# Sums of squares of two weight halves on ScalarE instead of Gram products on TensorE, in an adaptive-norm mixture-of-experts kernel

## The reference, cut to what matters

```python
out = einsum('bsi,io->bso', Efou * ys[:, None, :], weight) * d[:, None, :]
router_logits = y @ router_w.T + router_b + 0.1 * expert_weights
top_p, top_i = top_k(softmax(router_logits), 2)
top_p = top_p / top_p.sum(axis=-1, keepdims=True)
h = gelu(einsum('bsd,edh->bseh', y, w1) + b1, approximate=False)
expert_out = einsum('bseh,ehd->bsed', h, w2) + b2
x = x + (top_p[..., None] * take(expert_out, top_i)).sum(axis=2)
```

## Time and profile before

| what | value |
|---|---|
| median of 3 runs | 298.06 us (297.62 to 298.10) |
| the profiled execution | 296.99 us |
| its span | 295.2 us |
| its mean granted clock of TensorE | 0.965 of full |
| busy: PE / DVE / ACT / POOL | 269.6 / 191.9 / 195.2 / 175.4 us |
| read / written in HBM | 27.61 / 9.64 MB |

### The profile page before, as it was taken

The page is one execution under the profiler, slowest core; times in us unless marked ns, Lnnn a source line. Parts: engine busy times, 40 slices in busy tenths (PEclk is TensorE's granted clock), DMA queues, the critical chain, the costliest instruction groups (busy, mean ns, idle before and its releaser), DMA issues.

```text
span 295.2 us, 8972 instructions
## 1 busy us (share of the span) xinstructions
PE 269.6 (91%) x3065; PEld 221.2 (75%) x3065; DVE 191.9 (65%) x430; ACT 195.2 (66%) x425; POOL 175.4 (59%) x160
## 2 busy tenths in 40 slices
PE   7899967899999999999999999999999989999800
PEld 5778957788799998877778777777777767877500
DVE  2957787799999897656655655555656555556510
ACT  3355469499897997677667676766776756776500
POOL 8200026833366989887777877767787657464340
PEclk9799996999999999999999999999999999999985
DMA  6799995499862234645535555534535434332220
GB/s 160 290 400 388 368 323 155 129 404 450 294 191 41 38 59 69 95 76 88 93 56 91 75 93 73 79 68 76 90 59 80 88 56 74 53 39 25 32 35 1
DMA packets 39881, 39.53 MB, mean 134 GB/s; under 512 B 19920, under 2 KB 35744, under 8 KB 39680
## 3 DMA queue, kind: packets, MB, share of 16 engines
q1 hardware_dynamic: 32320, 28.56, 31.7%
q0 software_dynamic: 7488, 10.39, 21.9%
q10 hardware_dynamic: 32, 0.01, 0.0%
HBM read 27.61 MB, written 9.64 MB: 126 GB/s over the span
## 4 chain that ended last, share of the span: by engine, by line
PE 73%; DVE 9%; issue 6%; DMA 5%; POOL 4%; ACT 0%; DVEq 0%; POOLq 0%
PE ps L639 30%; PE ps L656 28%; DVE wsp L940 5%; PE ps L537 5%; DMA out<-onehot,idx 4%; PE ps L555 3%; POOL out L468 2%; PE ps L648 1%; POOL onehot L459 1%; PE ps L479 1%; PE ps L615 1%; DMA rows<-y_rows,idx 1%; PE ps L510 1%; PE ps L519 1%; DVE dv L871 1%
## 5 line engine op out<-in xcount | busy, mean ns | idle before, releaser
L639 PEld LDWEIGHTS ps<-onehot,wsp 128*128 (+1 forms) x1872 | 130.0, 98 | 37.4 <-issue 2.9
L639 PE MATMUL ps<-onehot,wsp 128*128 128x128 f16 x1872 | 154.4, 219 | 1.8 <-issue 1.5
L818 ACT ACTIVATE pay<-ps,cur 128x128 f32<-128x128 f32 x312 | 117.5, 463 | 54.9 <-issue 39.9
L656 PE MATMUL ps<-wsp,pay 128*128 (+1 forms) x616 | 139.4, 316 | 1.2 <-DVE pay L1102 1.2
L468 POOL DMA_INDIRECT out<-onehot,idx x39 | 68.7, 1762 | 28.9 <-POOL onehot L459 12.1
L1102 DVE SCALAR_TENSOR_TENSOR pay<-pay,cur 128x512 f16<-128x512 f32 x72 | 54.9, 762 | 28.8 <-ACT pay L806 26.6
L437 POOL DMA_INDIRECT rows<-y_rows,idx x39 | 49.4, 1266 | 22.4 <-issue 11.0
L459 POOL TENSOR_SCALAR onehot<-onehot,cur 128x256 f32<-128x256 f32 x37 | 43.0, 1161 | 25.6 <-DVE onehot L1120 21.6
L656 PEld LDWEIGHTS ps<-wsp,pay 128*128 128x128 f16 x616 | 45.3, 97 | 5.0 <-issue 1.6
L1096 DVE TENSOR_SCALAR pay<-pay,cur 128x512 f16<-128x512 f32 x36 | 19.4, 538 | 26.4 <-ACT pay L818 24.1
L806 ACT ACTIVATE pay<-pay,cur 128x512 f16<-128x512 f32 x36 | 26.0, 722 | 1.2
(11 more groups left out here) (177 smaller groups left out, 193.0 us busy)
## 6 DMA issues: line engine op xcount, KB each, us to landing
stage<-in_L_ffn_w SPq DMA_DIRECT2D x9, 1024.0 KB, 9.9
wsp<-in_L_ffn_w SPq DMA_DIRECT2D x7, 1024.0 KB, 11.8
y_rows<-pay SPq DMA_DIRECT2D x4, 512.0 KB, 9.4
wsp<-in_x SPq DMA_DIRECT2D x3, 512.0 KB, 8.1
b2bc<-in_L_ffn_b SPq DMA_DIRECT2D x1, 1024.0 KB, 9.4
rows<-y_rows,idx POOLq DMA_INDIRECT x39
out<-onehot,idx POOLq DMA_INDIRECT x39
wsp<-in_x SPq DMA_DIRECT2D x2, 256.0 KB, 5.8
```

The costliest lines, as they stand in the source:

```text
L639: last = mm(ps[:, HB + (2 * j + g) % RING, c * P:(c + 1) * P], wsp[:, bass.ds(e, 1), o:o + P].rearrange("p a f -> p (a f)"), xsp[:, j % RI ...
L656: last = mm(ps[:, OB + j % 2, 0:width], hsp[:, (2 * j + g) % NH, part, c, :], wsp[:, bass.ds(e, 1), o + w:o + w + width].rearrange("p a f ...
L818: last = a.activation(to, ps[:, HB + (2 * j + g) % RING, c * P:(c + 1) * P], ACT.Gelu, bias=cur[:, j % CURS, cc:cc + 1], scale=cur[:, j % ...
```

## The change

Group 6 (halves 14 and 15) has no Gram product any more. ACT squares each half as it lies in its place, 2048 float32 in a partition, with a running sum into its column of wsum: half 14 in turn 3, half 15 in turn 4, each in ACT's program ahead of that turn's split_high. PE drops gram(6) and DVE drops gram_max(6). At the end of turn 4 PE waits for both squares (and for the earlier users of the bank), then does sum_squares(6), and DVE does scale_weights(6) behind rows_out and low_h of turn 4, the place in its program where it was before. The sum is now the whole sum of squares of a half, where it was a sum of row maxima of the Gram product.

```diff
-GRAMS = {4: 4, 7: 5, 9: 6}
+GRAMS = {4: 4, 7: 5}
+SQUARED, SQUARES, SCALES = 6, {7: (14,), 9: (15,)}, 10
...
+        sqjunk = sb("sqjunk", [P, HALF], F8)
...
             def sum_squares(g):
-                if g < EARLY_GROUPS:
+                if g == SQUARED:
+                    pe.wait_ge(w_squared, len(GROUPS[g]))
+                elif g < EARLY_GROUPS:
...
                 if 2 * j + 2 in GRAMS:
                     gram(GRAMS[2 * j + 2])
+                if 2 * j + 2 == SCALES:
+                    for h in range(SQUARED):
+                        if GRAM_BANKS[h] == GRAM_BANKS[SQUARED]:
+                            pe.wait_ge(w_raw if h < EARLY_GROUPS else w_scaled[h], h + 1 if h < EARLY_GROUPS else 1)
+                    sum_squares(SQUARED)
...
+            def squares(n):
+                act.wait_ge(w_in[PLACE[n]], 16 * (len(earlier(n)) + 1))
+                k = column(n)
+                a.activation(sqjunk[:, :], staged_flat(n), ACT.Square, accum_out=wsum[:, k:k + 1],
+                             saturate=False).then_inc(w_squared, 1)
...
                 if j + 2 < XACT:
                     copy_x(j + 2)
+                for n in SQUARES.get(2 * j + 1, ()):
+                    squares(n)
                 for n in HIGHS.get(2 * j + 1, ()):
                     split_high(n)
...
                 if 2 * j + 2 in GRAMS:
                     gram_max(GRAMS[2 * j + 2])
+                if 2 * j + 2 == SCALES:
+                    scale_weights(SQUARED)
```

More of the change, by code:

```diff
@@ L239, in adaln_moe @@
         te_ready = sem("te_ready")
-        w_sq = sem("w_sq"); w_max = sem("w_max"); w_raw = sem("w_raw"); w_rounded = sem("w_rounded")
+        w_sq = sem("w_sq"); w_squared = sem("w_squared"); w_max = sem("w_max"); w_raw = sem("w_raw"); w_rounded = sem("w_rounded")
         gram_done, w_psum, w_scaled, w_t = (
```

## The result

| | before | changed |
|---|---|---|
| median, first measurement | 297.84 us (4 executions, 297.35 to 298.10) | 302.42 us (4, 301.06 to 304.52) |
| median, the run after_again below | 298.39 us (35, 296.21 to 301.23) | 303.06 us (12, 299.42 to 305.10) |
| the profiled execution | 296.99 us, span 295.2 | 301.06 us, span 299.3 |

The change makes the kernel slower: ratio 1.0162, 95% interval 1.0091 to 1.0232, in the first measurement, and 1.0112, 1.0070 to 1.0154, in the second. The direction was forecast, the size was not: 300.2 us was predicted and 302.0 was the upper end.

What follows compares the result with a forecast made beforehand. PE was taken to bound the kernel, with ACT's nearly solid program leaving no slack at two PE waits. The median 298.06 plus PE's shift of 2.1 us, which includes 1.0 from turn 3, gave 300.2 us; range 299.0 to 302.0.

Steps and rivals of the forecast that it cites:

- What bounds the kernel: PE's chain, with two waits without slack: gram_max(5) before sum_squares(5), 0.05 us; split_low(14) before tile 7's up matmuls, none.
- The price of a square: ACT, turns 3 and 4: each square with its accumulator read takes 2.0 us start to start, ends 1.9 and 2.2.
- The wait for half 14: ACT, turn 3: the square of half 14 waits 0.9 us for its load, ends 0 and 1.5.
- Step 1: Turn 3: split_high(12) moves by 2.9 us, PE waits 2.85 at sum_squares(5) and is 1.0 late after turn 4.
- Step 2: Turns 4 to 6: PE waits another 1.0 us for a late split_low(14); its shift becomes 2.1 us.
- What follows turn 6: After tile 7's first up matmuls: split_low(15) has 2 us to spare, so nothing is added.
- After 112 us: PE is busy 142.41 of 144 us at full clock, so its turn 6 shift is the end's shift.
- The clock: Turn 3: PE's 2.85 us idle may bring 6.8 us of half clock, costing 0.7 or 2.4 more; chance 0.25.
- The range: Whole kernel: 299.0 us with no load wait and cheap squares, to 302.0 with long ones and 0.5 for the clock.
- W: ACT's wait in turn 3 for half 14's load, ahead of its square: 0.9 us, ends 0 and 1.5.
- rival on the clock: Slower still, by half clock after PE's idle time in turn 3: 300.9 us, up to 302.6; chance 0.25.
- The base: Whole kernel before the change: median 298.06 us, 1.07 above the profiled execution, to which the shift was added.

Runs made afterwards that it cites:

- after_again: The changed kernel unedited, measured once more for its scatter; median 303.06 us over 12, ratio to before 1.0112.
- no_squares: The changed kernel without its two squares, sum_squares(6) adding group 5's columns instead; median 297.88 us, ratio to before 0.9970.
- filled: The changed kernel with eleven dummy matmuls in PE's program just ahead of sum_squares(5); median 300.91 us, ratio to before 1.0079.
- first_square_behind: Against the changed kernel: only half 14 squared, behind split_high(12) in turn 3, half 15 keeping its Gram product; median 299.48 us, ratio 1.0044.
- after_third: The changed kernel unedited, run for a further profile; 215.67 us from gram(5) to the end.
- layout_only: The kernel before with the added tensor and semaphore declared but never used; median 298.51 us, ratio to before 0.9998.
- squares_behind: The changed kernel with each square behind that turn's split_high instead of ahead; median 299.16 us, ratio 1.0018.
- squares_added: The kernel before, gram(6) and gram_max(6) kept, with the two squares added at the change's places, results unread; median 305.02 us, ratio 1.0228.
- first_square_only: Against the changed kernel: only half 14 squared, ahead of split_high(12), half 15 keeping its Gram product; median 304.93 us, ratio 1.0220.
- squares_twice: The kernel filled, here with 20 dummy matmuls, with each square done twice; four times from 302.08 to 308.30 us, ratio to before 1.0195.

## Why the prediction was wrong in size

- **What bounds the kernel: right.** Both points without slack were the ones named, and a third was missed (below). no_squares shows the second from the other side: PE's saving alone runs into split_low(14).
- **The price of a square: right.** 1.91 us from start to start against 2.0.
- **The wait for half 14: right in the first profile, wrong as a range.** 0.88 against 0.9. But over the profiles with the square ahead of the split, ACT's idle before it was 0.57 to 2.5 us, and I had 0 to 1.5, from two loads of one execution. Most of it goes to PE through gram_max(5), but not all: with 0.95 us more in after_again sum_squares(5) came 0.52 us later than in the first profile, with 1.33 more in filled 0.91, since ACT had come to the square earlier against gram(5) there.
- **Step 1: right.** split_high(12) moved by 2.90 us against gram(5) (82.55 - 82.84 = -0.29 before, 86.81 - 84.20 = 2.61 after), 2.9 forecast. PE was 13.14 - 12.09 = 1.05 us late after turn 4, 1.0 forecast.
- **Step 2: right in its result, partly by luck.** The second wait was 1.12 us long, 1.0 forecast; PE's shift at tile 7's up product is 20.31 - 18.14 = 2.17 us, 2.1 forecast. Inside it two misses cancel: split_low(14) started 2.51 us late against gram(5) (98.23 - 82.84 = 15.39 before, 102.10 - 84.20 = 17.90 after), 2.3 forecast, and it took 2.35 us where I had something between that and 2.69.
- **What follows turn 6: the step of the sum that failed, +0.5.** "I add nothing for it" looked at split_low(15) alone, and "nothing behind takes a delay in" was taken to cover the rest. At tile 8's up product the shift is 2.73 us, with PE idle for 0.40 us on issue. PE's register load for tile 8's expert (line L297 before, L299 after) starts at 105.5 us before and at 109.7 after, each time about 0.5 us behind the end of DVE's copy_x(8) (105.1 and 109.2). PE's transposes of tile 9 wait for that copy, and the load stands behind them, so a late copy leaves no time to do it under the matmuls. That is read from two timelines; filled has 0.21 us of the same idle time, and no run took the load away.
- **After 112 us: right for the changed kernel.** 2.73 us at tile 8 are 2.66 at the end. It is not exact in general: no_squares lost 0.4 and first_square_behind 0.5 us between tile 8 and the end.
- **The clock: the chance was wrong, the mechanism right, the price too high.** The prediction gave the fall 0.25; two of the three profiles of the changed kernel have it. It also said that the wait in turn 6 hides most of what the fall costs, and that is so: turn 4 took 2.67 us longer in after_again and the end was an estimated 1.1 us later for the fall of 6.8 us, where 2.4 was forecast, and 0.1 later for the fall of 3.4 in after_third, where 0.7 was forecast.
- **The range: the other step that failed.** Its upper end of 302.0 had W up to 1.5 (measured up to 2.5) and 0.5 for the clock, although the prediction's own rival on the clock went to 302.6, so the range did not hold what the text held possible. And it had no term at all for what happens ahead of gram(5), where the three profiles of the changed kernel lie 1.36, 3.00 and 3.85 us behind the one profile that served as base. Of the 1.96 us by which the profiled execution missed its forecast (301.06 against 299.1), 1.36 lie there and 0.56 behind gram(5).
- **The base.** 298.06 was the median of three; that of 35 is 298.39. That is 0.3 of the miss.

An estimate for the medians, from the table: 298.4 + 3.3 (from gram(5) on, the middle one of the three profiles: 2.7 as in the first, 0.6 more for a later half 14 and a short fall) = 301.7 us, against 303.06 measured (302.42 in the first four executions). The 1.4 us left lie ahead of gram(5). Whether the change has a hand in them is open. layout_only says that the layout has none. The same sum for squares_behind and filled, whose programs are the same as the changed kernel's up to turn 3, leaves -0.5 and -0.7 us, which speaks for chance; no run took the scatter of the start away.

## What to carry to other kernels

A share of busy time says nothing about whether an engine can take more work: look at what stands behind the place of the new instruction in the same queue, and how long before its reader each of those ends. ACT, at 66% and off the chain, had 0.05 us to give ahead of split_high(12) in turn 3, and behind it the square cost PE no wait there. When a forecast contains an idle stretch of PE of several microseconds, take the half clock after it as likely and not as a tail, look for later waits that hide its cost, and take the scatter of the base from dozens of executions before giving a range of one per cent.

## What the runs showed of the hardware that I had not expected

- In five profiles PE waited long at sum_squares(5) with nothing to do. A wait of 2.73 us (the first profile of the changed kernel) left the clock at 2.4 GHz. With waits of 2.41 us (squares_added), 3.24 (after_again), 3.28 (after_third) and 3.93 (first_square_only) it fell to 1.2 GHz, for 6.8, 6.8, 3.4 and 3.4 us, so the length of the wait decides neither whether it falls nor for how long. In first_square_only it fell only at 92.4 us, 1.3 us after the wait had ended. In the six profiles without a wait of over 0.9 us in turns 3 and 4 it did not fall there. The Trainium skill, page "TensorE: Matmul & The Clock Gate", section "HAM oscillation — how this bites in real kernels", warns of idle gaps of PE from which it returns cold. The traces agree in four of the five. In the profiles of filled and squares_twice, with dummy matmuls in the wait, it did not fall.
- The start varies by itself: in the profiles of all versions gram(5) starts anywhere from 82.56 to 87.24 us, 4.7 us apart, which is more than the change costs from gram(5) on in any of its three. The time at half clock before it goes from 3.4 us (filled) to 20.4 (squares_twice), but it is not all of it: filled, with the least, has gram(5) at 84.66.
- The time from issue to landing of the same 1 MB load (half 14) went from 7.3 us (squares_behind) to 10.3 (after_again) between profiles.
